# Second layer of a four-layer token mixer: the last gated expert outputs are added by VectorE, and one weight conversion is spread over other work

## The reference, cut to what matters

```
x = x + conv_branch_l(layernorm_c(x))          # l = 0..3, layer 3: depthwise 3x3
t = tokens(x)
logits = layernorm(t) @ router; probs = softmax(logits); top 2 of 8 experts, gates g[n, e]
# layers 0, 1:  every expert is computed for every token, most gates are zero
t = t + sum_e g[:, e] * (gelu(ln(t) @ W1[e] + b1[e]) @ W2[e] + b2[e])
# layers 2, 3:  only the two chosen experts of each token
t = t + sum_k g[:, k] * ((silu(ln(t) @ w1[e_k].T) * (ln(t) @ w3[e_k].T)) @ w2[e_k].T)
```

## Time and profile before

| what | value |
|---|---|
| median of 3 runs | 2315.94 us (2314.86 to 2321.67) |
| profiled execution, its own time | 2319.88 us |
| its span in the trace | 2318.0 us |
| mean granted TensorE clock | 0.815 of full speed |
| busy share PE / DVE / ACT / POOL | 70% / 74% / 59% / 43% |

### The profile page before, as it was taken

How to read it: one execution, slowest core, us unless ns; L and a number is a source line. 1 busy time by engine, 2 the same in 40 slices (tenths; PEclk the granted TensorE clock), 3 DMA queues, 4 the chain that set the end, 5 groups by cost and what they waited for, 6 DMA issues and landing times.

```text
span 2318.0 us, 50893 instructions
## 1 busy us (share of the span) xinstructions
PE 1612.0 (70%) x16820; PEld 1202.0 (52%) x16821; DVE 1704.9 (74%) x2874; ACT 1361.0 (59%) x2473; POOL 1000.0 (43%) x955
## 2 busy tenths in 40 slices
PE   4367777768676777667667933699924199978995
PEld 3334444435343444336666822588823088867884
DVE  3567767776877677546777878788866588869886
ACT  0256655676778575775555731477711277766774
POOL 1024334432223122882222467244477677754443
PEclk8588857788887676997788965799955599989997
DMA  7000000000001000000000010000020211110002
GB/s 302 0 25 1 1 25 1 1 1 1 1 1 74 25 1 2 22 21 20 17 17 18 27 56 23 23 27 28 22 83 23 93 37 33 34 63 23 27 28 88
DMA packets 53029, 76.27 MB, mean 33 GB/s; under 512 B 14905, under 2 KB 37642, under 8 KB 50206
## 3 DMA queue, kind: packets, MB, share of 16 engines
q1 hardware_dynamic: 30658, 43.26, 5.9%
q0 software_dynamic: 22208, 30.81, 3.8%
HBM read 40.89 MB, written 35.19 MB: 33 GB/s over the span
## 4 chain that ended last, share of the span: by engine, by line
PE 33%; DVE 16%; issue 5%; POOL 5%; ACT 2%; DMA 2%; POOLq 0%; SPq 0%; ACTq 0%; DVEq 0%
PE bank L1634 12%; PE bank L1635 9%; PE bank L1648 5%; POOL rows L581 3%; PE bank L1650 2%; DVE tmp L1083 2%; PE bank L1620 1%; DVE act L1243 1%; DVE hl L1247 1%; PE bank L1388 1%; POOL x L619 1%; PE bank L1530 1%; ACT act L789 1%; DVE st L907 1%; DVE tmp L1060 1%
## 5 line engine op out<-in xcount | busy, mean ns | idle before, releaser
L605 POOL DMA_INDIRECT y<-ysb,ids x352 | 394.2, 1120 | 519.3 <-DVE ysb L1234 446.4
L619 POOL TENSOR_TENSOR x<-x,ysb 128x256 f32<-128x256 f32 x288 | 266.1, 924 | 670.4 <-DVE ysb L1321 661.9
L771 ACT ACTIVATE hb<-bank,bias_sb 128x512 f32<-128x512 f32 x432 | 299.4, 693 | 246.3 <-issue 138.7
L1634 PE MATMUL bank<-xT,gA 128*114 128x256 f16 x1056 | 331.3, 314 | 59.1 <-DVE act L1243 28.5
L581 POOL DMA_INDIRECT rows<-rowsb,pos x288 | 328.6, 1141 | 98.6 <-issue 74.6
L1243 DVE TENSOR_TENSOR act<-bank,act 114x512 f32<-114x512 f32 x352 | 241.6, 686 | 164.1 <-ACT act L789 163.7
L789 ACT ACTIVATE act<-bank 114x512 f32<-114x512 f32 x352 | 210.2, 597 | 234.9 <-PE bank L1635 230.9
L1635 PE MATMUL bank<-xT,uB 128*114 128x256 f16 x1056 | 299.6, 284 | 0.0
L1634 PE MATMUL bank<-xT,uA 128*114 128x256 f16 x1056 | 299.5, 284 | 0.0
L1635 PE MATMUL bank<-xT,gB 128*114 128x256 f16 x1056 | 299.3, 283 | 0.0
L1648 PE MATMUL bank<-dW,hl 114*128 x2112 | 260.1, 224 | 7.1 <-DVE hl L1247 6.2
(11 more groups left out here) (246 smaller groups left out, 3410.6 us busy)
## 6 DMA issues: line engine op xcount, KB each, us to landing
xs<-rows SPq DMA_DIRECT2D x176, 65.0 KB
stage<-up SPq DMA_DIRECT2D x8, 1368.0 KB, 6.6
rows<-land POOLq DMA_DIRECT2D x8, 1137.5 KB, 18.1
y<-ysb,ids POOLq DMA_INDIRECT x352, 2.2
rows<-rowsb,pos POOLq DMA_INDIRECT x288, 2.3
stage<-down SPq DMA_DIRECT2D x2, 1368.0 KB
rowsb<-y SPq DMA_DIRECT2D x4, 640.0 KB, 6.3
rows<-land POOLq DMA_DIRECT2D x4, 585.0 KB, 20.7
```

Source lines behind the costliest of these rows:

```text
L605: pool.indirect_dma_start(y_d[h], bass.IndirectOffsetOnAxis(ids[h][:, t * SUB + u:t * SUB + u + 1], 0), ysb[t % UNROLL][:, u * C:(u + 1) * ...
L619: pool.tensor_tensor(xv, xv, tg[u % 2], ALU.add).then_inc(s["added"], 1)
L771: ins = a.activation(dst[:, 0:SPAN * P], PB[w % 3][:, :], ACT.Gelu, scale=1.0 / WSCALE, bias=b1T[l][:, at:at + 1])
L1634: pe.matmul(PB[bank][0:CH, o], w[0][:, at], xT[k][:, :], start=True, stop=False)
```

## The change

It has three parts.

1. From unit 32 (`PLACED`) of (1, 1) on, DVE does the add itself: instead of one 128x256 multiply into `tg`, it issues four multiply-adds of 128x64 (`scalar_tensor_tensor`) from PSUM into `x[h]`, with the gate as a scalar per partition. POOL does no add after unit 31 and sends the 72 rows of (2, 0) one behind the other. PE reuses a PSUM bank after `added` instead of `gated`.
2. `wprep` of layer 3 is woven into `prep(3, 1)` by the new helper `beside`: pieces 0 and 1 ahead of it, piece 2 after the first layer norm, piece 3 inside the convolution, piece 4 after the second layer norm. SP loads two pieces early instead of one.
3. `EARLY` goes from 30 to 4, so 68 instead of 42 sends of (3, 1) are spread over the tiles of `back(3, 0)`.

```diff
@@ -38,7 +38,7 @@
 SUB = ROWS // P
 UNROLL = 4
 INNER = 24
-EARLY = 30
+EARLY = 4
 TILES = -(-((TOPK * NTOK + E * (ROWS - 1)) // ROWS) // UNROLL) * UNROLL
 WORD = 7
 MAXE = -(-NTOK // ROWS)
@@ -396,10 +396,23 @@
             used = n * 45 // 100 if (l, h) == (1, 1) else n - 4
             return [todo[min(len(todo), -(-(v + 1) * len(todo) // used)) - 1] for v in range(n)]
 
+        PLACED = weave(1, 1).index(next(k for k in weave(1, 1) if k >= ROUTE + 20)) // 2 + 4
+
+        def direct(l, h, u):
+
+            return (l, h) == (1, 1) and u >= PLACED
+
         def tile_base(l, h):
             return m_of(l, h) * TILES
 
         NSLOT = TILES * G
+
+        def beside(steps, weights):
+
+            for at, k in ((LN1 - 1, 1), (LN1 + 9, 2), (CONV + 15, 3), (LN2 + 9, 4)):
+                steps.upto(at)
+                weights.upto(WPREP + 3 * k + 2)
+            steps.upto(LAST)
 
         def inner(l, h):
 
@@ -494,7 +507,7 @@
             sp.wait_ge(s["stage_used"], 1)
             sp.dma_start(b2p[1:2, :], b2[:, 2 * E * C:4 * E * C]).then_inc(s["b2_moved"], 16)
             load_stage(2, range(PIECES))
-            load_stage(3, range(1))
+            load_stage(3, range(2))
 
             def moe(l, h):
                 n, tb = m_of(l, h), tile_base(l, h)
@@ -539,12 +552,12 @@
                         sp.dma_start(returned(l, h)[k][:, t0:t1, :], src).then_inc(y_in[h][p], 16)
 
             for l in range(SPARSE, NL):
-                if l == 3:
-                    load_stage(3, range(1, PIECES))
                 for h in range(HALVES):
                     moe(l, h)
                     if (l, h) != (NL - 1, 0):
                         bring(l, h)
+                if l == SPARSE:
+                    load_stage(3, range(2, PIECES))
             for h in range(HALVES):
                 for p, (t0, t1) in enumerate(PARTS):
                     sp.wait_ge(s["combined"], NP * m_of(NL - 1, h) + p + 1)
@@ -608,24 +621,22 @@
                 for _ in aside:
                     pass
 
-            def dense(l, h, aside, begin):
+            def dense(l, h):
 
                 ub = unit_base(l, h)
                 for u in range(NUNIT):
                     s8 = u // E
                     xv = x[h][:, s8 * SPAN:(s8 + 1) * SPAN, :].rearrange("p t c -> p (t c)")
+                    if direct(l, h, u):
+                        return
                     pool.wait_ge(s["gated"], ub + u + 1)
                     wait_from(pool, s["added"], ub + u)
                     pool.tensor_tensor(xv, xv, tg[u % 2], ALU.add).then_inc(s["added"], 1)
-                    if u >= begin:
-                        next(aside, None)
-                        next(aside, None)
-
-            placed = weave(1, 1).index(next(k for k in weave(1, 1) if k >= ROUTE + 20)) // 2 + 4
+
             first = scatter(SPARSE, 0)
             for l in range(SPARSE):
                 for h in range(HALVES):
-                    dense(l, h, first, placed if (l, h) == (1, 1) else NUNIT)
+                    dense(l, h)
             for _ in first:
                 pass
             back(2, 0, iter(()), 0)
@@ -852,9 +863,8 @@
             moe(2, 0, Woven(after(2, 0)))
             Woven(prep(3, 0)).upto(LAST)
             moe(2, 1, None)
-            Woven(prep(3, 1)).upto(LAST)
             a.wait_ge(s["y_done"], tile_base(3, 0))
-            Woven(wprep(3)).upto(LAST)
+            beside(Woven(prep(3, 1)), Woven(wprep(3)))
             for h in range(HALVES):
                 moe(3, h, None)
 
@@ -1316,6 +1326,14 @@
                     s8, e, c = todo[k]
                     u = s8 * E + e
                     v.wait_ge(s["down_ps"], vb + k + 1)
+                    if direct(l, h, u):
+                        v.wait_ge(s["added"], ub + u)
+                        for t_ in range(SPAN):
+                            xt = x[h][:, s8 * SPAN + t_, :]
+                            ins = v.scalar_tensor_tensor(xt, PB[3 + (ub + u) % 3][:, t_ * C:(t_ + 1) * C],
+                                                         gd[h][:, s8 * SPAN + t_, e:e + 1], xt, ALU.mult, ALU.add)
+                        ins.then_inc(s["added"], 1)
+                        return
                     wait_from(v, s["added"], ub + u - 1)
                     g = gd[h][:, s8 * SPAN:(s8 + 1) * SPAN, e]
                     v.tensor_tensor(tg[u % 2].rearrange("p (t c) -> p t c", c=C),
@@ -1359,8 +1377,7 @@
             moe(2, 0, Woven(after(2, 0)))
             Woven(prep(3, 0)).upto(LAST)
             moe(2, 1, None)
-            Woven(prep(3, 1)).upto(LAST)
-            Woven(wprep()).upto(LAST)
+            beside(Woven(prep(3, 1)), Woven(wprep()))
             moe(3, 0, None)
             moe(3, 1, Woven(joined(NL - 1, 0)))
             Woven(joined(NL - 1, 1)).upto(LAST)
@@ -1579,7 +1596,7 @@
                     w, u = vb + k, s8 * E + e
                     y = PB[3 + (ub + u) % 3]
                     if c == 0:
-                        wait_from(pe, s["gated"], ub + u - 2)
+                        wait_from(pe, s["added" if u >= 3 and direct(l, h, u - 3) else "gated"], ub + u - 2)
                         row = b2p[:, (l * E + e) * C:(l * E + e + 1) * C].unsqueeze(1).broadcast_to([2, SPAN, C])
                         pe.matmul(y[:, 0:SPAN * C], one16[0:2, :], row, start=True, stop=False, skip_group_check=True)
                     pe.wait_ge(s["lo_ready"], w + 1)
@@ -1671,7 +1688,7 @@
 
                 pe.wait_ge(s["route_ready"], n_of(l, h) + 1)
                 if (l, h) == (SPARSE, 0):
-                    pe.wait_ge(s["gated"], unit_base(SPARSE, 0))
+                    pe.wait_ge(s["added"], unit_base(SPARSE, 0))
                 turn_rows(0, 0, 0)
                 turn_rows(0, 1, 0)
                 body23(0, first=True)
```

## The result

| | before | with the change |
|---|---|---|
| median | 2315.4 us (2313.65 to 2321.67, 4 runs) | 2282.24 us (2279.34 to 2283.47, 4 runs) |
| profiled execution, span | 2318.0 us | 2280.2 us |

The ratio is 0.985 (95%: 0.9829 to 0.9871), 33 us less; 28 were forecast. The two spans lie 37.8 us apart, since the profiled execution of before took 2319.88 us, 4.5 above its median.

What follows compares the result with a forecast made beforehand. It took POOL's adds and sends to bound the end of (1, 1) and of moe(3, 0), and weight pieces to delay moe(3, 0)'s start. 20 + 23 - 15 = 28 us gave a 2288 us median; range 2267 to 2304.

Steps and rivals of the forecast that it cites:

- rival 2: In (1, 1), DVE becomes the bound at 3.04 us a unit; total gain 13 us, 2303 us; chance 0.10.
- DVE gets as busy here as in moe, so I take 1.11: Row sends of (2, 0) during (1, 1): 1.11 us each, pitch 1.41, last start at 1022.7, a gain of 20 us.
- The whole return, with combine behind it, comes 4.8 us late: After moe(2, 1): POOL's last tile send, held by weight pieces 0 and 1, ends about 1699.3 instead of 1694.5.
- rival 3: Late return and blocked (3, 0) sends make rows the gate of moe(3, 0); total gain 18 us, 2298 us; chance 0.07.
- rival 1: In moe(3, 0) POOL keeps up, loss 0 to 5 us; total gain 40 us, 2275 us; chance 0.20.
- (4): Sends in moe(3, 0) at a pitch over 1.60 us make the kernel slower; at 1.70, 2331 us; chance 0.04.
- POOL then paces moe(3, 0): In moe(3, 0) DVE's evicts queue for four ysb buffers and PE waits behind; 5.0 us a tile, loss 15 us.
- C: Stretch from moe(3, 0)'s first product to PE's first transposes of moe(3, 1); its forecast loss was 15 us, range 0 to 21.

Runs made afterwards that it cites:

- e7_two_wide: The changed kernel with each direct add as two 128x256 instructions instead of four 128x64 ones; 2280.54 us, ratio 0.9847 to the kernel before.
- e8_two_pieces: The changed kernel with only weight pieces 0 and 1 ahead of combine, 2 to 4 behind prep(3, 1); 2296.4 us, ratio 0.9917 to the kernel before.
- e6_rows_first: The changed kernel with EARLY at 12 and the other 60 rows spread over the first 38 tiles, not 44; 2258.02 us, ratio 0.9745 to the kernel before.
- e1_direct_only: The kernel before with only the direct adds; weights behind prep(3, 1) and EARLY 30 as before; 2292.11 us, ratio 0.9904.
- e3_early30: The changed kernel with EARLY back at 30 instead of 4; 2274.56 us, ratio 0.9824 to the kernel before.
- e2_weights_no_direct: The changed kernel without direct adds: POOL does all adds and paired sends, weights woven in, EARLY 4; 2302.16 us, ratio 0.9949 to the kernel before.
- e4_early12: The changed kernel with EARLY at 12 instead of 4; 2272.0 us, ratio 0.981 to the kernel before.

## Why the prediction was right

**Part 1, direct adds (20 forecast, 25.6 measured).** The mechanism held: no unit waits for POOL, and the last send sets the start. That DVE is no bound (rival 2) is shown by ACT's 10.00 in the windows; the four adds hold DVE for 0.77 us, between the 0.56 and 0.9 worked out; e7_two_wide shows that their form is of no weight. The step that failed is "DVE gets as busy here as in moe, so I take 1.11". DVE did get as busy, 8.97 of 10 (42 of 50 in moe(3, 0)), yet sends took 1.036 us, and from first to last 95.8 us for 100.6: 4.8 us of the 5.6. So DVE's busy share does not by itself set the length of a send; what does was not found. The adds' starts lie 0.19 to 0.20 us apart, inside the 0.14 to 0.23 forecast.

**Part 2, the weights (23 forecast, 27.3 measured).** Pieces 2, 3 and 4 took 3.0, 3.0 and 3.4 us as priced, and no piece stands before the first product. "The whole return, with combine behind it, comes 4.8 us late" was wrong: the send ended 0.9 us after the first of the two pieces, between them, and combine came 1.1 late. That is 3.7 of the 4.3 us that B was better. Here the forecast leaned on one send that had met two pieces at another moment of its own run. e8_two_pieces shows the two shares: 10.2 us from the first two pieces, 17.1 from the other three. The row sends did not become a gate (rival 3): the last one of (3, 0) starts at 1777.28, PE's first transposes only at 1787.76.

**Part 3, EARLY (15 forecast as a loss, 18.5 measured; 15.8 alone).** 152 sends in 216.3 us were forecast and 218.2 measured, a pitch of 1.43 for 1.42; that is 1.9 us of the 3.5, and 1.3 more are the first return, 13.2 us after the first product for 11.9. (Before, the sends in that stretch were 127 and not 128, which enters no term.) The rivals that POOL keeps up (1) or that sends take 1.60 and more (4) fell with that. But "POOL then paces moe(3, 0)" is wrong: a tile took 4.74 us and not 5.0 (on the mean up to the 34th, the same as before), and DVE, for which PE was to wait, lacked a buffer only in the last tiles (5.6 us in all, 3.4 of them when PE had finished); the lag is stored in four buffers and comes due as idle time of PE before moe(3, 1). The number came out right because the last row was the end in either view. That part is luck. The difference matters for the remedy: if POOL had paced every tile, only fewer sends would have helped, while in truth the same sends in another order (e6_rows_first) give 24 us. Nor is the loss EARLY's alone, as the sum has it. With EARLY = 30 C grows from 217.5 (e1_direct_only) to 230.2 (e3_early30) when the weights move forward, because POOL is then still at its 30 sends when the first tiles are ready; 10.9 us of it are the wait of the fifth evict shown above. EARLY = 4 adds 5.4 to that, and 15.8 where the weights stand as before. So part 2 gives 27 us at its own place and costs 12.7 of them in the next stage.

**The sum.** Forecast 20 + 23 - 15 = 28, measured 33 (median), 37.8 between the profiled spans. The two gains were 4 to 6 us too low and the loss 3.5 too low, so the errors cancel in part. The median of 2282 us lies 6 us from the 2288 forecast and 7 from the 2275 of rival 1: the number alone doesn't tell the two apart, PE's 22 us of idle time does. The stretches measured apart (e1_direct_only and e2_weights_no_direct, 23 and 13 us) confirm that these two gains and one loss are the whole of it. That S is 2.1 us shorter with the change is inside what other kernels show there (617.8 to 620.1).

## What to carry to other kernels

- In these traces an engine that lagged behind a pipeline with buffers cost next to nothing until the buffers were full or until something at the end waited for its last item. Price a lag at both ends, and look at what stands last in its queue: here returns could wait and rows could not, and putting the rows first was worth more than half as much as the whole change.
- An engine's idle time beside a round trip through DRAM was the cheapest place for work from elsewhere: two conversions there cost 1.1 us for 10 saved.
- A second engine may have lived on the time that a repair removes. Here POOL sent rows while the weights were converted, and 12.7 of the 27 us won came back as its lag.
- Cut every trace at the same few events and compare the pieces. Executions reached the first cut up to 9 us apart here, which would have hidden most single effects.

## What the runs showed of the hardware

In these traces a send that started 0.2 us or more into a long DVE instruction with two SBUF inputs was held until that had ended, but it matters when it starts. The four traces in which a row send started 0.28 or 0.29 us into the first of two 3 us weight pieces that follow each other show 6.46 us each time, held through both (e8_two_pieces below). In the nine traces with two pieces behind the last evict the last return started 1.0 to 1.3 us into the first piece, and took 2.61 to 2.86 us: it ended 0.9 us after the first piece. And a send that had started 0.12 us before the piece, at 1663.00 above, took its usual 0.98, as did five in other traces that started 0.01 to 0.02 us into it.

```profile
1787.38 6.46 POOL L593 DMA_INDIRECT rows<-rowsb,pos  x1 [0.30 <-issue]
```

The Trainium skill (SBUF — State Buffer, "Who interferes with whom") says that such an instruction and a POOL instruction that reads SBUF contend for a port under an exclusive lock, and infers that descriptor generation, which writes, is spared by it. The rows agree with the first. Against the second they show less than the prediction said: these sends are held, but each also takes its row numbers (`pos`, `ids`) from SBUF, so it may be that read and not the generation of descriptors that waits. No run separates the two. Why a send goes through between two pieces in one phase and not in another stays open; no experiment moved the phase on purpose.

Short instructions of that kind do far less: `low` is one (0.69 us, two in each unit), and with DVE 90% busy 49 of the 72 sends of (2, 0) with the change took 0.95 to 0.98 us, as with little beside them.

ACT's gelu took 0.71 us on the mean beside the four multiply-adds, 0.695 before, and 0.69 beside the two wide instructions of e7_two_wide (fp32 groups in 920 to 1018 us: 710, 695 and 690 ns). It cost nothing: a unit took 2.32 us in both, from the first to the last of the 40 adds. That both engines read PSUM at that time is a possible cause, not a shown one.

PE's granted clock goes with a difference of over 1 us at the start of moe(3, 0). In the six traces in which it was 1.00 from 5 to 10 us after the first product, the first evict came 10.2 to 10.8 us after that product; in the six with 0.84 to 0.88 it came after 11.8 to 12.0. Kernels with the same code up to there (e4_early12 and e6_rows_first) fall on both sides.
